# A four-batch fused transformer kernel: the last batch's transform summed by tile pairs, its spectrum read from PSUM, two FiLM tiles on VectorE, and a new written-out order

## The reference, cut to what matters

```python
x = x + cross_attention_16_heads(layernorm(x), ctx)            # block 0
x = x + top2_of_8_experts_ffn(layernorm(x))                    # block 1, "moe"
t = layernorm(x)                                               # block 2, "text"
attn_mean = mean over 4 heads of softmax over the 32 largest of 77 scores
c_t = attn_mean @ V
u = layernorm(t) * (1 + gate*scale_in(c_t)) + gate*shift_in(c_t)     # FiLM in
y = irfft(rfft(u, n=1024) * rfft(K, n=1024))[:512] + u * D_skip      # long convolution
y = y * (1 + gate*scale_out(c_t)) + gate*shift_out(c_t)              # FiLM out
xt = t + y;  xt = xt + gelu(layernorm(xt) @ W1 + b1) @ W2 + b2;  x = x + layernorm(xt)
q  = int8 quantisation of layernorm(x), times an int8 quantised 128x128 matrix   # block 3
x  = x + dequantised product
```

## Time and profile before

| what | value |
|---|---|
| median of 3 runs | 533.92 us (533.39 to 535.6) |
| the profiled execution: its time / its span | 530.86 us / 529.0 us |
| PE busy | 464.2 us (88%) |
| DVE busy | 422.4 us (80%) |
| ACT busy | 257.1 us (49%) |
| POOL busy | 118.0 us (22%) |
| mean granted TensorE clock | 0.952 of full |

### The profile page before, as it was taken

How to read it: one execution, slowest core, us unless ns; L and a number is a source line. 1 busy time by engine, 2 the same in 40 slices (tenths; PEclk the granted TensorE clock), 3 DMA queues, 4 the chain that set the end, 5 groups by cost and what they waited for, 6 DMA issues and landing times.

```text
span 529.0 us, 9306 instructions
## 1 busy us (share of the span) xinstructions
PE 464.2 (88%) x3050; PEld 365.7 (69%) x3057; DVE 422.4 (80%) x1761; ACT 257.1 (49%) x548; POOL 118.0 (22%) x193
## 2 busy tenths in 40 slices
PE   4727578999999999999999999999999999758861
PEld 3316416899769989747988789759869888436750
DVE  4889997846337857978999998998798699995667
ACT  3626477754644565634447645543575434721040
POOL 6820113210200210004022243100225220342021
PEclk9968599999999999999999999999999999968996
DMA  7510293021000040000004000000000000000000
GB/s 202 67 30 2 71 334 102 2 40 22 2 2 2 1 60 1 4 2 0 2 1 60 2 1 1 24 1 1 1 2 2 4 18 2 0 1 21 1 0 20
DMA packets 16179, 14.69 MB, mean 28 GB/s; under 512 B 1211, under 2 KB 14275, under 8 KB 16132
## 3 DMA queue, kind: packets, MB, share of 16 engines
q1 hardware_dynamic: 16132, 14.11, 11.7%
HBM read 8.79 MB, written 1.05 MB: 19 GB/s over the span
## 4 chain that ended last, share of the span: by engine, by line
PE 72%; DVE 18%; issue 3%; ACT 3%; POOL 3%; DMA 1%; DVEq 0%; POOLq 0%; ACTq 0%
PE moe_y L959 20%; PE moe_h L947 20%; PE side L1015 4%; PE side L904 3%; PE side L906 3%; PE side L1003 3%; PE side L1025 2%; PE side L1068 2%; PE side L1046 2%; DVE area L1452 2%; PE side L803 1%; PE side L983 1%; PE side L1034 1%; PE side L865 1%; PE moe_h L969 1%
## 5 line engine op out<-in xcount | busy, mean ns | idle before, releaser
L1179 ACT ACTIVATE HT<-moe_h,W 128x256 f32<-128x256 f32 x256 | 115.4, 473 | 103.0 <-PE moe_h L947 102.5
L947 PE MATMUL moe_h<-xnT_moe,W 128*128 128x256 f32 x512 | 136.4, 382 | 1.0 <-ACT xnT_moe L1121 0.8
L959 PEld LDWEIGHTS moe_y<-W,HT 128*128 128x128 f32 x1024 | 131.0, 191 | 8.7 <-issue 1.4
L959 PE MATMUL moe_y<-W,HT 128*128 128x128 f32 x1024 | 135.6, 276 | 0.2 <-DVE X L1425 0.2
L947 PEld LDWEIGHTS moe_h<-xnT_moe,W 128*128 128x128 f32 x512 | 87.5, 191 | 14.5 <-issue 6.9
L1425 DVE SCALAR_TENSOR_TENSOR X<-moe_y,RW,X 128x128 f32<-128x128 f32 x128 | 38.6, 345 | 12.9 <-PE moe_y L959 12.1
L1452 DVE MATCH_REPLACE8 area<-TOP,area 128x77 f32<-128x77 f32 x192 | 40.9, 231 | 0.0
L1756 POOL TENSOR_TENSOR area<-area 128x128 f32<-128x128 f32 x16 | 7.3, 458 | 109.9 <-ACT area L1209 109.9
L1439 DVE MAX8 TOP<-area 128x8 f32<-128x77 f32 x192 | 31.5, 231 | 0.0
L1366 DVE TENSOR_REDUCE mx<-side 128x6 f32<-128x462 f32 (+1 forms) x48 | 24.9, 579 | 8.1 <-PE side L865 8.1
L969 PE MATMUL moe_h<-W 128*128 128x256 f32 x112 | 30.0, 428 | 0.0
(11 more groups left out here) (325 smaller groups left out, 827.7 us busy)
## 6 DMA issues: line engine op xcount, KB each, us to landing
W<-in_w SPq DMA_DIRECT2D x8, 512.0 KB, 8.4
QA<-Q SPq DMA_DIRECT2D x24, 128.0 KB, 4.1
X<-in_x SPq DMA_DIRECT2D x4, 256.0 KB, 7.3
KM<-area SPq DMA_DIRECT2D x6, 160.0 KB, 5.2
out_dram<-FO SPq DMA_DIRECT2D x3, 256.0 KB, 2.3
V<-in_vpack SPq DMA_DIRECT2D x1, 579.0 KB, 9.7
area<-in_gpack SPq DMA_DIRECT2D x1, 576.0 KB, 6.0
FW<-in_dftf SPq DMA_DIRECT2D x1, 512.0 KB, 7.0
```

Source lines behind the costliest of these rows:

```text
L947: pe.matmul(moe_h[n % 2][:, 0:HS], W1[:, e, c * P:(c + 1) * P], xnT_moe[:, b % 2, h * HS:(h + 1) * HS], start=True, stop=True).then_inc(mo ...
L959: mm = pe.matmul(moe_y[m % 2][:, t * P:(t + 1) * P], HT[:, m % 2, c, t * P:(t + 1) * P], W2[:, e, c, :], start=(c == 0), stop=(c == HC - 1))
L1179: act.activation(HT[:, m % 2, c, :], moe_h[n % 2][:, 0:HS], ACT.Relu, bias=wc("b1")[:, e * HC + c:e * HC + c + 1]).then_inc(moe_h_ready, 1)
```

## The change

1. `dft` (all batches): both banks are reserved first, and tile pair `k` is now the outer loop. Pair 0 (tiles 0 and 2) may start once tile 2 is there, pair 1 waits for tile 3. One bank's matmuls form a single start/stop group.
2. `direct(b)`, true for the last batch: ScalarE no longer copies the two `dft` banks; VectorE reads them in PSUM.
3. `spectrum` (all batches): the four products with the real part come first and wait only for its bank, then the four with the imaginary part, then the six sums. It has 14 operations as before, of the same sizes. `idft` starts its first two products when YR is done and its last two when YI is.
4. `film` of tiles 2 and 3 of the last batch: no ScalarE copy (L1209) and no GpSimd; VectorE multiplies and adds, out of PSUM.
5. `late_steps`: batch 2's last five quantisation steps leave stream O and become the start of stream Z.
6. `ORDER` is new from end to end.

```diff
+def direct(b):
+    return b == LAST
@@ needed
+    if kind == "idft" and b == LAST and i == 0:
+        return [former, late_steps()[-1]]
+    if step == late_steps()[0]:
+        return [("ln_apply", b, "out")]
+def late_steps():
+    return half_steps(LAST - 1, 0)[-5:]
@@ streams
-        "O": [s for b in range(B) for s in tail_steps(b)],
-        "Z": half_steps(LAST, 1),
+        "O": [s for b in range(B) for s in tail_steps(b) if s not in late_steps()],
+        "Z": late_steps() + half_steps(LAST, 1),
@@ tensor: dft
-                        pe.wait_ge(xm_ready, T * (b + 1))
+                    for k in range(2):
+                        if kind == "dft":
+                            pe.wait_ge(xm_ready, T * b + T - 1 + k)
+                        for n in range(2):
+                            dst, full = outs[n]
+                            for q in range(2):
@@ tensor: idft
-                    pe.wait_ge(y_a, 14 * (b + 1))
+                    for r in range(4):
+                        pe.wait_ge(y_a, 12 * b + (10 if r < 2 else 12))
@@ scalar
+                    if summed(b, i):
+                        act.wait_ge(xm_ready, n + 1)
+                    else:
                         act.activation(FAB[:, i % 2, :], src[:, 0:2 * D], ACT.Copy).then_inc(fab_ready, 1)
-                if kind == "dft":
+                if kind == "dft" and not direct(b):
@@ vector: film, last batch, tiles 2 and 3
+                    dve.tensor_tensor(XM[:, i, :], xn4[:, i, :], src[:, 0:D], ALU.mult).then_inc(film_mul, 1)
+                    dve.wait_ge(film_mul, n + 1)
+                    dve.tensor_tensor(XM[:, i, :], XM[:, i, :], src[:, D:2 * D], ALU.add).then_inc(xm_ready, 1)
@@ vector: spectrum
+                    dve.tensor_tensor(Ya[:], xr, bc(KR), ALU.mult).then_inc(y_a, 1)
+                    dve.tensor_tensor(Yb[:], xr, bc(KI), ALU.mult).then_inc(y_a, 1)
+                    dve.tensor_tensor(Yc[:], xr[:, :, 0, :], KR[:, :, 1, :], ALU.mult).then_inc(y_a, 1)
+                    dve.tensor_tensor(Ye[:], xr[:, :, 0, :], KI[:, :, 1, :], ALU.mult).then_inc(used[0], 1)
...
+                    dve.tensor_tensor(YR[:], xi, bc(KI), ALU.mult).then_inc(y_a, 1)
```

More of the change, by code:

```diff
@@ L226 @@
+E C E2 C E O T2 E3 T E O E2 O T C2 U5 T7 O T2 O T O T6 W2 T Z W2 Z T2 O Z2 O W7 Z O4 Z3 O2 Z2 O Z O2 W O Z2 O Z2 O
+Z2 O W Z O Z W
 """
@@ L1484, in _ @@
                                                      ALU.mult, ALU.add).then_inc(top_acc, 1)
-                if kind == "spectrum":
-                    emptied(dve, "dft", b, 0, 0)
-                    emptied(dve, "dft", b, 0, 1)
+                if kind == "film" and summed(b, i):
+                    n = b * T + i
+                    src, read = filled(dve, kind, b, i)
+                    dve.wait_ge(n4_ready, HN * b + i // HT_ + 1)
+                    dve.wait_ge(xm_ready, n)
+                    dve.tensor_tensor(XM[:, i, :], xn4[:, i, :], src[:, 0:D], ALU.mult).then_inc(film_mul, 1)
+                    dve.wait_ge(film_mul, n + 1)
+                    dve.tensor_tensor(XM[:, i, :], XM[:, i, :], src[:, D:2 * D], ALU.add).then_inc(xm_ready, 1)
@@ new lines, in _, with bc @@
+                if kind == "spectrum":
+                    def bc(k):
+                        return k[:, :, 0:1, :].broadcast_to((P, 2, NB, D))
+                    xs, used = [], []
+                    for q, x in enumerate((XR, XI)):
+                        if direct(b):
+                            x = bank("dft", b, 0, q)[:].rearrange("p (c k d) -> p c k d", c=2, k=NB)
+                        xs.append(x)
+                        used.append(side_read[FILL[("dft", b, 0, q)][0]] if direct(b) else x_used)
+                    xr, xi = xs
+                    n = 12 * b
+                    if direct(b):
+                        filled(dve, "dft", b, 0, 0)
+                    else:
+                        emptied(dve, "dft", b, 0, 0)
@@ L1508, in _ @@
-                    dve.tensor_tensor(Ya[:, :, 1, :], XI[:, :, 0, :], KD[:, :, 1, :], ALU.mult).then_inc(y_a, 1)
-                    dve.wait_ge(y_a, n + 9)
                     dve.tensor_tensor(YR[:, :, 1, :], YR[:, :, 1, :], Yc[:], ALU.add).then_inc(y_a, 1)
+                    if direct(b):
+                        emptied(dve, "dft", b, 0, 0)
+                        emptied(dve, "dft", b, 0, 1)
+                    else:
+                        dve.wait_ge(x_used, 2 * (b + 1))
+                    dve.tensor_tensor(Ye[:], Ye[:], Yf[:], ALU.add).then_inc(y_a, 1)
@@ L1748, in _ @@
                         .then_inc(xb_ready, 1)
-                if kind == "film":
+                if kind == "film" and not summed(b, i):
                     n = b * T + i
-                    pool.wait_ge(fab_ready, n + 1)
+                    pool.wait_ge(fab_ready, plain_until(n) + 1)
                     pool.wait_ge(n4_ready, HN * b + i // HT_ + 1)
```

71 lines of the change are left out of this document (32 added, 39 removed).

## The result

The changed kernel takes 528.94 us (median of 7 runs, 527.7 to 531.25), the kernel before beside it 533.51 us (7 runs, 532.47 to 535.6). The ratio is 0.9926, 95% interval 0.9906 to 0.9945: 0.74% faster, about 4 us (the two medians are 4.6 us apart). The time lies inside the range, on its low side, and 5.4 us under the forecast of 534.3. The likeliest case, no change, was wrong. The profiled execution took 529.95 us with a span of 526.6.

What follows compares the result with a forecast made beforehand. VectorE's order was taken to bound the head, TensorE the middle, one chain through TensorE, VectorE and GpSimd the end. 4.5 + 1.1 - 5.7 = -0.1 us, plus 0.5 for the tail's warm steps, gave 534.3 us, range 528.5 to 540.

Steps and rivals of the forecast that it cites:

- The likeliest case, no change: Whole kernel: a median of 534.3 us, no change from 533.92; chance 0.42, range of this case 531.3 to 536.5.
- The head: +4.5 us: Before the experts: nine warm steps ahead of `norm_T` delay VectorE's work up to 79.43 us; bounds +2.9 to +13.
- The middle: +1.1 us: Expert stretch: two steps moved ahead of the last expert matmul add 0.9 us on a full TensorE, new idle time 0.2.
- give nothing back: Head: the eight warm steps that left their place between the score maxima save nothing, having run beside VectorE's table work.
- The extra warm step behind `norm_T`: Head, `norm_T` of "moe": this step (0.88 us) outlasts ScalarE's copy (0.6) by some 0.15 us.
- bounds for the stalls: Middle: a new order can add TensorE idle time, taken as +0.2 us, from -1 to +4.
- The tail: 5.7 us: After the last expert add, M: the first FiLM-out operation comes at M+42.7 instead of M+48.39, a gain of 5.7 us.
- The price of 5.39 us: Tail, `dft`: 5.39 us for 16 before, at a clock of 0.58; 3.6 us taken for the new one.
- the early real part: Tail: spectrum can't start early, as VectorE waits for `quant_T`; were it to start under `dft`, another 1.5 us would go.
- the head costs little: Rival: head only +1 to +3 us, tail gain stays, 531.3 us or 529; chance 0.30 with a better tail.
- The clock falls in the last tail: Rival: without the warm step between `norm_T30` and `ffn_up30` the clock falls, costing 1.8 us, 536 us; chance 0.08.
- New stalls in the middle: Rival: new TensorE stalls of 2 to 4 us in the expert stretch, 537 us; chance 0.10.

Runs made afterwards that it cites:

- the third trace of the kernel before: The kernel before with nothing changed, one more execution profiled: 533.89 us, span 532.0, first expert matmul at 93.9.
- the new head alone: The kernel before with only the new order up to the first expert matmul: 534.98 us, ratio 1.0036 to the kernel before.
- the second and third trace: The kernel before, unchanged, profiled twice more: 530.28 us (span 528.4) and 533.89 us (span 532.0).
- without the early pair: The changed kernel, but in all batches the first tile pair of `dft` also waits for tile 3: 531.05 us, ratio 0.9971 to the kernel before.
- the moved warm step: The kernel before with one warm step moved from ahead of `smax3` to between `score04` and the first product: 531.11 us, ratio 1.0001.
- the old order under the new code: The changed kernel with the order of before up to `moe_up(3,(1,2,0))`, the new one behind it: 529.85 us, ratio 0.9939 to the kernel before.
- the early spectrum: The changed kernel with VectorE's `quant_T` and `quant_mm` behind the spectrum and two warm steps behind `idft`: 525.64 us, ratio 0.9881 to the kernel before.

## Why the prediction was wrong

**Two terms of the sum failed. The larger is "The head: +4.5 us", as a difference to be added to the median.** Its own working held: the warm steps of the first block took 5.55 us (forecast 6.0), those of the second 2.75 (2.65), `kgen_base` 0 came at 19.80 us (20.5) and the first expert matmul at 95.97 (95.5). But "all of VectorE's work up to 79.43 us hangs behind it" was read from one execution that was quicker than most: it took 530.86 us where the median is 533.5. The sum was made against it and the result then added to the median, as if the missing time lay in a place that the change doesn't touch. It lies in the very stretch that was priced. In the third trace of the kernel before the clock stays at half beyond 70 us, the first products take double, and VectorE waits 2.84 us for them. A VectorE that comes later fills this wait instead of moving the end. Against that trace, the new head moves the reciprocal by 1.18 us (82.30 to 83.48) and not by 4.05, with 0.67 us of the wait left, and the first expert matmul by 2.1 us. **The other is "The middle: +1.1 us"**, which measured -0.5 us, and -0.9 up to M: 2.0 us off, nearly as much. The tail and the rest are right to 0.3 us against the same trace, once its own slow `ffn_up` is taken off.

The remaining 0.92 us of the head's lateness was not foreseen and has its row in the changed kernel's trace, TensorE's timeline at 87 us:

```profile
87.78 2.05 PE L933 MATMUL side<-W,qr 128*128 128x128 f32 x8 [1.45 <-DVE qr L1403]
```

In the profile before these eight took 1.13 us. The windows of 87 to 91 us show a granted clock of 0.57, after an idle gap of 1.45 us; the trace of the new head alone has the same 2.05 us in this place. It is not the rule: the five other kernels that were traced with this head have 1.13 us there, and their first expert matmul comes at 94.25 to 94.84 us, 0.4 to 1.0 us behind the third trace of before. In those five the reciprocal starts at 82.7 to 83.1 us and waits for nothing: VectorE is 3.3 to 3.6 us late, and the 2.84 us of wait absorb most of it. The prediction counted eight warm steps that left their place; the orders have ten. One of the two that it missed stood just ahead of these eight matmuls (82.18 us in the profile before, with a gap of 0.41 us behind it instead of 1.45), the other among the scores at 64.49 us. That they "give nothing back" was not tested. What the traces show is that with the old head three of seven have the products at 70 us at full clock, with the new head none of seven.

The extra warm step behind `norm_T`, to which the prediction gave 0.15 us, costs nothing: `norm_T` starts 1.41 us ahead of the first expert matmul in both kernels (94.56 to 95.97, and 89.59 to 91.00).

The Trainium skill, page "TensorE: Matmul & The Clock Gate", section Part 1, has the low clock as the default which continuous work lifts. The trace agrees: TensorE has 0.03 us of work from 24 to 35 us, and the granted clock is 0.50 in the windows from 30 to 77 us. So the twenty warm instructions at 6.6 us buy nothing there.

**The sum against an ordinary execution.** From the third trace of before (span 532.0) to the changed kernel's:

| part | predicted | measured against the profile before | against the ordinary trace |
|---|---|---|---|
| first expert matmul | +4.5 | +4.97 | +2.10 |
| first to last expert matmul | +1.1 | -0.48 | -0.49 |
| last expert matmul to M | 0 | -0.37 | -0.37 |
| M to the start of `idft` | -5.7 | -6.86 | -5.99 |
| from there to VectorE's last instruction | +0.5 | +0.44 | -0.61 |
| sum | +0.4 | -2.3 | -5.4 |

The last column is a single pair, and 1.05 us of its sum is the third trace's own slow `ffn_up` (the last row would be +0.44 without it). That leaves -4.3, which fits the ratio's -4 and the medians of the spans (526.7 against 530.9). The time around the span differs too: it was 3.35 us in the changed kernel's profiled execution and 1.9 in all three traces of before, and this is not explained here.

**The middle: +1.1 us, measured -0.5.** The sign was wrong by 1.6 us. The two moved steps are there (2475 matmuls between the first and the last expert matmul; 2470 in the second and third trace of before), and yet the stage is shorter. The "2.9 us of idle time" of the prediction was misread: 0.8 us of it lies behind the last expert matmul (449.75 to 451), and 0.8 us more belongs to six matmul records that this trace lacks (2464). In the second and third trace TensorE's idle time in the stage is 1.26 us, and in the changed kernel's 1.06. One wait of 0.2 us (L959, for VectorE) is gone; the busy time fell from 357.50 to 357.22 us although five instructions came in. So the added work costs nothing that can be seen, but the runs do not show where the rest of the 0.5 us comes from; the cause stays open. Seven traces with the new middle have 358.2 to 358.4 us, and the eighth, without the early pair, 359.5; the three of the kernel before and that of the new head alone have 358.75 to 358.76. The prediction's bounds for the stalls (-1 to +4) hold this value, and it took the other side without a row for it. That M lies another 0.37 us nearer to the last matmul follows from `topk` 312, which no longer stands between the last adds.

**The tail: 5.7 us, measured 6.0 to 6.9.** Point by point from M: the last `topw` at +25.7 (forecast 25.8), `am_T` of tile 3 at +27.0 (27.6, the extra for a low clock was not needed), the FiLM table at +29.6 (30.2), `dft` done at +33.1 (33.8), the spectrum at +33.7 (34.8; `quant_T` takes 0.6 behind `dft`, forecast 1.0), `idft` at +39.5 (40.7), FiLM-out at +41.5 (42.7). The mechanism is right in each step; the sum was 1.2 us too cautious. The price of 5.39 us for the `dft` before was itself one execution's: two other traces have 3.72, the trace of the new head alone 5.40.

**The unknown costs.** Reading PSUM costs nothing, as the rows said. The wait for `quant_T` that hides the early real part is shown from both sides (the early spectrum gains 1.1 us up to `idft`). Of the tail's parts the moved quantisation carries 1.3 us by the trace (2 by the times) and the early pair 1.0, with 1.2 more in the middle, where the prediction gave it nothing; FiLM on VectorE and the direct read carry none. The top-k round that moved ahead of M (1.4 us by the forecast) was not tried by itself.

**The rivals.** What happened is closest to "the head costs little": 531.3, or 529 with a better tail. Its reason was another one, though. The early clock did not come up; the cost was swallowed by a wait that the profile before did not show. "The clock falls in the last tail" was real in four of the traces with the new tail, at 0.8 to 1.9 us, though not in that of the changed kernel. It is not tied to the warm step that is gone: the third trace of before and that of the moved warm step have this step and lose 1.05 us there. "New stalls in the middle" did not come in the changed kernel; they came with the old order under the new code (1.15 us) and without the early pair (1.0 us).

## What to carry over

Where the profiled execution is quicker or slower than the median by as much as the change is worth, look for where the two differ before anything is added to the median, and take a second trace; a cost on one engine counts only down to the wait of another that the ordinary execution has. When a data path is opened by finer waits, look at what stands between producer and consumer in both engines' orders: moving `quant_T` behind the spectrum brought `idft` 1.1 us forward, as much as the early pair did. Compare windows from one event to the same event, and two traces of one kernel, before a wait is called gone: missing records look like waits. Warm work delays what stands behind it where TensorE's queue feeds the engine that sets the pace: here 9.3 us of it, with four moved steps, made VectorE 3.6 us later.

## What was not expected of the hardware

The same kernel shows its stretches at half clock in different places from one execution to the next. Between the second and third trace of the kernel before (spans 528.4 and 532.0) this is nearly all of the difference. Around 70 us it costs 2.9 us (reciprocal at 79.43 or 82.30), and by the spans most executions have it; under `dft` 1.7 us (5.39 or 3.72); at `ffn_up` around 500 us 0.8 to 1.9 us; at the first expert matmuls 6.3 us in the one trace that has it, and the times of four of the twelve runs of that kernel fit it. Ahead of the fall TensorE had a gap or two, from 0.8 us each to nearly six us without work ahead of 56 us, but the same gaps stand in other traces without a fall, so the gap alone does not decide. The granted clock in the record is 1.0 for the first 24 us of the changed kernel, yet the first twenty warm instructions took 0.278 us each on average, against 0.221 at full clock: there the record says less than the durations do.
